# A four-block graph network on one core: node stages pipelined by tile and laid beside the passes over the edges

## The reference, cut to what matters

```python
# block 0: messages
s, v = x[:, :32] @ lin1_s, einsum(x[:, 32:], lin1_v)        # node product
w = silu(edge_attr_8 @ fc1) @ fc2                            # per edge, 8 -> 64 -> 128
ns, nv = segment_sum(products of w, s[src], v[src], edge_attr_4, by dst)
out = concat([ns @ lin2_s, nv @ lin2_v])                     # node product
# block 1: three convolutions with layernorm and elu, then a fourth
c = segment_sum((h @ W)[src] * dinv[src] * dinv[dst], dst) + b
h = elu(layernorm(c * sigmoid(a)) * g + beta)
# block 2: mean over neighbours, by src
mean = segment_sum(x[dst], src) / max(count, 1)
out = relu(x @ W_self + b_self + (mean @ W_neigh + b_neigh if count > 0))
# block 3: attention with two heads
e = leaky_relu(a_src[src] + a_dst[dst]); alpha = softmax of e over the edges of a dst
out = prelu(segment_sum((x @ W_src)[src] * alpha, dst) + bias)
```

## Time and profile before

| | |
|---|---|
| median of 3 runs | 10167.17 us (10166.1 to 10173.07) |
| the profiled execution | 10193.51 us, span 10191.7 us |
| PE busy | 6004.4 us (59%) |
| DVE busy | 5701.8 us (56%) |
| ACT busy | 2635.3 us (26%) |
| POOL busy | 6861.4 us (67%) |
| mean granted TensorE clock | 0.779 |
| HBM traffic | 75 GB/s over the span |

### The profile page before, as it was taken

One profiled execution on the slowest core, in us unless ns is written; L12 is line 12 of the kernel. 1 busy time (PEld: TensorE's weight loads), 2 busy tenths in 40 slices (PEclk: granted clock), 3 DMA queues, 4 the chain that ended last, 5 costly groups with the idle time before them and its releaser, 6 DMA issues. The chain is left out here.

```text
span 10191.7 us, 104956 instructions
## 1 busy us (share of the span) xinstructions
PE 6004.4 (59%) x23343; PEld 4243.9 (42%) x23343; DVE 5701.8 (56%) x15117; ACT 2635.3 (26%) x8724; POOL 6861.4 (67%) x7083
## 2 busy tenths in 40 slices
PE   0676745555766665666656666555554443477775
PEld 0343423333544443444434444333343333366664
DVE  9306047777455556555565555544443333599998
ACT  0332345555222223111121111100010000366663
POOL 0677757777177774777657775577767777177774
PEclk9999977777588886888878888777765555688886
DMA  7111123334022232333323333333332222222222
GB/s 260 50 58 48 58 76 99 102 102 91 25 52 52 52 50 73 100 101 101 83 85 100 100 100 72 94 101 100 100 78 52 53 52 52 35 48 48 48 48 39
DMA packets 350525, 773.48 MB, mean 76 GB/s; under 512 B 120740, under 2 KB 181816, under 8 KB 343336
## 3 DMA queue, kind: packets, MB, share of 16 engines
q0 software_dynamic: 251328, 600.99, 23.9%
q1 hardware_dynamic: 91176, 108.80, 3.8%
q10 hardware_dynamic: 7488, 57.94, 1.5%
HBM read 615.60 MB, written 151.68 MB: 75 GB/s over the span
## 5 line engine op out<-in xcount | busy, mean ns | idle before, releaser
L573 DVE TENSOR_TENSOR acc<-acc,ps 128x256 f32 (+3 forms) x4992 | 1886.4, 378 | 2885.3 <-PE ps L870 2430.2
L870 PE MATMUL ps<-rows,hot 128*128 128x256 f32 (+2 forms) x5824 | 1651.9, 444 | 1792.6 <-issue 947.9
L749 POOL DMA_INDIRECT rows<-table_gcn,index_dst x2080 | 2078.7, 999 | 676.2 <-issue 600.8
L870 PEld LDWEIGHTS ps<-rows,hot 128*128 128x128 f32 x5824 | 1285.6, 273 | 2226.2 <-issue 1232.7
L791 ACT ACTIVATE ut<-u,fld 128x128 f16<-128x128 f16 x1664 | 576.7, 393 | 2757.7 <-DVE u L828 2756.5
L749 POOL DMA_INDIRECT rows<-table_gat,index_dst x832 | 923.0, 1109 | 464.5 <-issue 253.2
L492 POOL DMA_INDIRECT dst_rows<-pay,acc x782 | 798.6, 1021 | 529.6 <-ACT pay L476 305.4
L749 POOL DMA_INDIRECT rows<-table_lin,index_dst x832 | 872.8, 1049 | 335.0 <-issue 239.5
L749 POOL DMA_INDIRECT rows<-table_mean,index_src x832 | 803.7, 966 | 258.4 <-issue 253.3
L725 PE MATMUL ps<-prod,hot 128*128 128x260 f32 x1664 | 626.4, 541 | 559.4 <-issue 365.5
L856 PE MATMUL ps<-prod,ut 128*128 128x416 f16 x3328 | 888.6, 399 | 0.0
(11 more groups left out here) (259 smaller groups left out, 9274.3 us busy)
## 6 DMA issues: line engine op xcount, KB each, us to landing
dst_rows<-pay ACTq DMA_DIRECT2D x52, 1088.0 KB, 31.5
fld<-dst_rows SPq DMA_DIRECT2D x104, 544.0 KB, 3.7
rows<-table_gcn,index_dst POOLq DMA_INDIRECT x2080, 2.5
table_gcn<-acc SPq DMA_DIRECT2D x15, 1024.0 KB
rows<-table_lin,index_dst POOLq DMA_INDIRECT x832
rows<-table_mean,index_src POOLq DMA_INDIRECT x832, 2.5
rows<-table_gat,index_dst POOLq DMA_INDIRECT x832
dst_rows<-pay,acc POOLq DMA_INDIRECT x782, 2.3
```

The source lines that it names most:

```text
L573: c.nc.vector.tensor_tensor(to, to, product, ALU.add).then_inc(c.added.sem, 1)
L749: pool.indirect_dma_start(to(q, j), None, table, bass.IndirectOffsetOnAxis(ap=c.idx[k][:, t:t + 1], axis=0)).then_inc(c.gathered[q % per]. ...
L870: pe.matmul(c.ps[:, j % ahead, 0:used], c.hot[:, r % 2, j, :], row_of(c, s, r, j, used), start=True, stop=True).then_inc(c.mm.sem, 1)
```

## The change

1. **Scatter.** `scatter_dst` takes on the first node product, one tile per group of eight chunks, for the first 49 groups. SP's order becomes load of group q, store of tile q-1 into t0, load of group q+1. PE turns tile q ahead of the group's layers and multiplies tile q-1 behind them. ACT copies tile q back (`back`) and tile q-1 out (`take`) behind its payload copies. The node product and `write_table` behind the stage are gone.
2. **Messages to first convolution.** `degrees`, the node product, `normalise` and `ranges` become `message_glue`: `turn_tiles` with two halves and one 128-row weight matrix (`apart`), norm per cut on ACT, degree root by Newton steps on POOL, table per cut by SP. The message rows are 257 wide (`AU`) instead of 260.
3. **Roots.** `newton` has three iterations instead of four, for every cut root; `CUTS` has 45 where it had 46, `conv_glue` shifts by `due(k, 3)` and joins at the cut's fifth tile instead of its last.
4. **Mean.** `aggregate` by src also makes `x @ W_self + b_self` into `acc[:, tile, 132:260]`, turning or multiplying one tile on PE in alternate groups; sums use four PSUM banks instead of eight. SP sends the bins of the chunks through HBM, and DVE makes of them the penalties that `bin_starts` made.
5. **Mean to attention.** `mean_glue` runs everything from the mean's product to table t6 in one stage of 67 steps (49 tiles + `ROWS`): the norm of tile k-14, its turn at k-16, product at k-17, rows at k-18. POOL also clears `acc` by cut.
6. **Attention.** The destination's scores are listed once for all chunks (two transposes, four matmuls against a one-hot of the bins, four copies), and `node_scores` is one copy of eight chunks.
7. **End.** `add_gat` and `normalise` become `final_glue`: ACT divides by the sum of weights, DVE adds bias, prelu, x and statistics per cut, POOL the root, ACT the norm, SP the store, per cut.

The core of the diff:

```diff
+            def put(k, h):
+                sp.wait_ge(m.taken.sem, k + (m.taken.n + 1))
+                sp.dma_start(to[:, one(k), :], s.u[:, h:h + 1, 0:D]).then_inc(m.put[h].sem, 16)
+
+            def both(i, h):
+                load(i, h, G8)
+                if not (first(i) and h == 0):
+                    put(2 * i + h - 1, 1 - h)
...
+            with sp.Fori(1, half // 2) as i:
+                for h in range(2):
+                    both(i, h)
...
+            def turn(k, h):
+                if not (isinstance(k, int) and k < 2):
+                    pe.wait_ge(m.back.sem, k + (m.back.n - 1))
+                pe.transpose(c.ps[:, 4 + h, 0:P], c.x[:, one(k), :].rearrange("p a w -> p (a w)"),
+                             c.ident[:, :]).then_inc(m.turned.sem, 1)
+
+            def multiply(k, h):
+                pe.wait_ge(m.back.sem, k + (m.back.n + 1))
+                if not (isinstance(k, int) and k < 2):
+                    pe.wait_ge(m.taken.sem, k + (m.taken.n - 1))
+                pe.matmul(c.ps[:, 6 + h, 0:D], s.ut[:, h, 0:P], s.lin1[:, :], start=True,
+                          stop=True).then_inc(m.multiplied.sem, 1)
+
+            def both(i, h):
+                q = 2 * i + h
+                turn(q, h)
+                mlp(i, h, G8)
+                if q:
+                    multiply(q - 1, 1 - h)
...
+            def back(k, h):
+                act.wait_ge(m.turned.sem, k + (m.turned.n + 1))
+                if not (isinstance(k, int) and k < 2):
+                    act.wait_ge(m.multiplied.sem, k + (m.multiplied.n - 1))
+                nc.scalar.activation(s.ut[:, h, 0:P], c.ps[:, 4 + h, 0:P], ACT.Copy).then_inc(m.back.sem, 1)
+
+            def take(k, i, h):
+                act.wait_ge(m.multiplied.sem, k + (m.multiplied.n + 1))
+                if not (isinstance(k, int) and k < 2):
+                    act.wait_ge(m.put[h].sem, i * 16 + m.put[h].n)
+                nc.scalar.activation(s.u[:, h, 0:D], c.ps[:, 6 + h, 0:D], ACT.Copy).then_inc(m.taken.sem, 1)
+
+            def both(i, h):
+                q = 2 * i + h
+                payload(i, h, G8)
+                back(q, h)
+                if not (first(i) and h == 0):
+                    take(q - 1, i - (h == 0), 1 - h)
...
+            def own(k):
+                dve.wait_ge(m.multiplied.sem, m.multiplied.n + k + 1)
+                nc.vector.tensor_tensor(c.acc[:, k, OWN:OWN + D], c.ps[:, 6 + k % 2, 0:D], s.bself[:, :],
+                                        ALU.add).then_inc(m.taken.sem, 1)
...
+                if bins is not None and q % 2 == 0 and 2 <= q < 2 * NT + 2:
+                    own(q // 2 - 1)
+                if bins is not None and q == 9:
+                    penalties()
...
+            def turn(k):
+                if k >= 2:
+                    pe.wait_ge(m.back.sem, m.back.n + k - 1)
+                pe.transpose(c.ps[:, 4 + k % 2, 0:P], c.x[:, k, :], c.ident[:, :]).then_inc(m.turned.sem, 1)
+
+            def multiply(k):
+                pe.wait_ge(m.back.sem, m.back.n + k + 1)
+                if k >= 2:
+                    pe.wait_ge(m.taken.sem, m.taken.n + k - 1)
+                pe.matmul(c.ps[:, 6 + k % 2, 0:D], s.ut4[:, k % 4, 0:P], s.wself[:, :], start=True,
+                          stop=True).then_inc(m.multiplied.sem, 1)
...
+def newton(st, y, of, e):
+
+    eng = st.eng
+    for i in range(3):
+        st(eng.tensor_tensor(e, of, y, ALU.mult)).wait()
+        st(eng.tensor_tensor(e, e, y, ALU.mult)).wait()
+        st(eng.tensor_scalar(e, e, -0.5, 1.5, ALU.mult, ALU.add)).wait()
+        last = eng.tensor_tensor(y, y, e, ALU.mult)
+        if i < 2:
             st(last).wait()
-    last.then_inc(s.m.rooted.sem, 1)
+    return last
...
-                for j in due(k, 2):
+                for j in due(k, 3):
                     shifted(j)
                 if i:
                     measure(k - 1)
-                if g >= 2 and k == CUTS[g + 1] - 1:
+                if g >= 2 and i == min(4, CUTS[g + 1] - CUTS[g] - 1):
...
+def message_glue(c, s, table):
+
+
+    nc = c.nc
+    v, m = nc.vector, s.m
+    node = lambda k: c.x[:, k, :]
+    with nc.Block() as block:
+
+        @block.tensor
+        def _(pe):
+            turn_tiles(c, s, pe, lambda k: c.acc[:, k, 0:HID], 2, s.lin2, 2 * MUL, 2, apart=True)
+
+        @block.scalar
+        def _(act):
+            def normal(k):
+                g, i = cut_of(k)
+                if i == 0:
+                    act.wait_ge(m.centred.sem, m.centred.n + g + 1)
+                nc.scalar.activation(node(k), node(k), ACT.Identity, scale=c.rstd[:, k:k + 1],
+                                     bias=c.mv[:, k, 0:1]).then_inc(m.part.sem, 1)
+
+            for k in range(NT):
+                bring_back(c, s, act, k, HID)
+                g, i = cut_of(k)
+                if g >= 2:
+                    n, of = CUTS[g + 1] - CUTS[g], CUTS[g - 1] - CUTS[g - 2]
+                    for j in range(i * of // n, (i + 1) * of // n):
+                        normal(CUTS[g - 2] + j)
+            for k in range(CUTS[NCUT - 2], NT):
+                normal(k)
+
+        @block.vector
+        def _(dve):
+            st = Steps(dve, c.dve)
+
...
+            for k in range(NT):
+                g, i = cut_of(k)
+                if i == 0 and g:
+                    measure(k - 1)
+                    cut_moments(c, s, st, g - 1, D, -1.0)
+                bank = 2 + k % 2
+                dve.wait_ge(m.multiplied.sem, m.multiplied.n + k + 1)
+                v.tensor_tensor(node(k)[:, 0:MUL], node(k)[:, 0:MUL], c.ps[:, bank, 0:MUL], ALU.add)
+                vec = node(k)[:, MUL:D].rearrange("p (u i) -> p i u", i=3)
+                v.tensor_tensor(vec, vec, c.ps[:, bank, MUL:D].rearrange("p (i u) -> p i u", i=3),
+                                ALU.add).then_inc(m.taken.sem, 1)
+                if i:
+                    measure(k - 1)
+                if g == 2 and i == 0:
+                    dve.wait_ge(m.back.sem, m.back.n + k)
+                    dve.wait_ge(m.fed.sem, m.fed.n + 2)
+                    st(v.tensor_scalar(s.ndinv[:, :], c.dinv[:, :], -1.0, None, ALU.mult))
+                if g >= 3 and i == 0:
+                    rows(g - 3)
...
+            pool.wait_ge(m.fed.sem, m.fed.n + 1)
+            newton(st, c.dinv[:, :], s.degree[:, :], s.newton[:, :]).then_inc(m.fed.sem, 1)
+            pool.wait_ge(m.fed.sem, m.fed.n + 2)
+            for g in range(NCUT):
+                t = slice(CUTS[g], CUTS[g + 1])
+                cut_root(c, s, st, g)
+                pool.wait_ge(m.rooted.sem, m.rooted.n + g + 1)
+                pool.tensor_tensor(c.mv[:, t, 0], c.mv[:, t, 0], c.rstd[:, t], ALU.mult).then_inc(m.centred.sem, 1)
...
+NORMAL, TURN, MULTIPLY, ROWS = 14, 16, 17, 18
...
+            turn(0)
+            turn(1)
+            for k in range(NT + ROWS):
+                if k < NT:
+                    multiply(k)
+                if k + 2 < NT:
+                    turn(k + 2)
+                if 0 <= k - TURN < NT:
+                    turn_node(k - TURN)
+                if 0 <= k - MULTIPLY < NT:
+                    multiply_node(k - MULTIPLY)
...
+            for k in range(NT + ROWS):
+                if k < NT:
+                    back(k)
+                if 0 <= k - NORMAL < NT:
+                    normal(k - NORMAL)
+                if 0 <= k - ROWS < NT:
+                    rows(k - ROWS)
+                if 0 <= k - TURN < NT:
+                    node_back(k - TURN)
...
+            def take(k):
+                dve.wait_ge(m.multiplied.sem, m.multiplied.n + k + 1)
+                v.scalar_tensor_tensor(part(k), c.ps[:, 2 + k % 2, 0:D], s.rcnt[:, k:k + 1], c.acc[:, k, OWN:OWN + D],
+                                       ALU.mult, ALU.add).then_inc(m.taken.sem, 1)
+
+            def bias(k):
+                dve.wait_ge(m.taken.sem, m.taken.n + k + 1)
+                v.scalar_tensor_tensor(part(k), s.bneigh[:, :], s.has[:, k:k + 1], part(k), ALU.mult,
+                                       ALU.add).then_inc(m.shifted.sem, 1)
+
+            def residual(k):
+                dve.wait_ge(m.shifted.sem, m.shifted.n + k + 1)
+                v.scalar_tensor_tensor(node(k), part(k), 0.0, node(k), ALU.max, ALU.add).then_inc(m.cut.sem, 1)
+
+            def measure(k):
+                dve.wait_ge(m.cut.sem, m.cut.n + k + 1)
+                st(v.bn_stats(s.st6[:, k, :], node(k)))
+                g = cut_of(k)[0]
+                if k == CUTS[g + 1] - 1:
+                    cut_moments(c, s, st, g, D, -1.0)
...
+                pool.wait_ge(m.taken.sem, m.taken.n + CUTS[g + 1])
+                pool.memset(c.acc[:, t, :], 0.0)
...
+            act.wait_ge(m.fed.sem, m.fed.n + 1)
+            divided(0)
+            divided(1)
+            for g in range(NCUT):
+                if g + 2 < NCUT:
+                    divided(g + 2)
+                normal(g)
...
+            for g in range(NCUT + 1):
```

(34 more changed lines are left out.)

519 lines of the change are left out of this document (343 added, 176 removed).

## The result

The changed kernel took 9930.3 us (median of 4, 9927.1 to 9931.8), the kernel before 10166.6 in the same comparison: a ratio of 0.9766, 95% interval 0.9749 to 0.9783, 236 us less. Forecast were 9933 and 234 less. The two profiled executions differ by more, 10193.5 and 9927.1, spans 10191.7 and 9925.3: 266 us. The one of before was 26 us over its median, the one of after was not. Totals are therefore compared only within one chip or with before on it, and stages first of all on the chip that gave 10164 for before.

The account below looks back on a forecast made before the run. POOL's indirect DMA issues bound each pass, and stages between passes add their length. Terms 72-51-112-24-2+3-98+0-22 = -234 took the profiled 10193.5 us to 9959, less 26 to the median: 9933 us, range 9865 to 9990.

Parts of the forecast that it names:

- the last one of the sum: Whole kernel: 9959 us for a profiled execution, lowered by the 26 us it lay above the median, to 9933.
- The chain: Scatter: tile copies, store, next load, TensorE and payload copies in series, 11.8 us a group for 50 groups, +72 us.
- my estimate of waits and register steps: Scatter, per group: waits and register steps on SP and ACT, store's packets ahead of the load's, 0.45 us.
- The rival of the hidden chain: Scatter: TensorE at its higher level, chain some 8 us, pass stays at 1045, total 9861 us; chance 0.15.
- The rival on TensorE's clock: New stages after the messages and the mean: TensorE stays at 1.2 GHz, +17 and +25 us, total 9975; chance 0.10.
- The likely case: Messages to first convolution: TensorE not at its lower level, 66.5 us to the first gather, -112 us.
- no memsets (-1): Messages to first convolution: the new stage lacks the memsets of the one after the fourth convolution, 1 us less.
- the stage loses one iteration and one tile of tail work: After the fourth convolution: one root iteration fewer and one tile of tail work shifted, -2 us.
- Step and stall: Mean to attention: 1.25 us a step, and ACT standing 2.7 us for the root at six cuts, 16 us.
- POOL waits for nobody in it, so one copy for eight on DVE gives 0 there: Pass of attention: copying the scores once for eight chunks gains 0 us, bounds -15 to +15.
- waits 0.3: End: DVE's waits per eight tiles, 0.3 us of 7.9, in a stage of 63.6 us, -22 us.
- the rival of the blocked roots: Root steps on POOL blocked by two-input DVE work, 2 to 4 us more at each of 13 cuts, 9965 us; chance 0.07.

Follow-up runs that it names:

- three orders at once: Changed kernel with SP's load ahead of the store in the scatter, norm three steps later after the mean, division ahead at the end: 9833.5 us, 0.9677 of before.
- the two runs above: Changed kernel with four root iterations and eight score copies: 9978.0 us; changed kernel with the old shift and join order, own product left out: 9937.1 us.

## Why the prediction was right, point by point

**The total was right partly by two errors that met.** The terms of the sum made 234 us where the traces have 266. The other step that failed is the last one of the sum, which took the 26 us between the profiled execution and the median of before as an offset that the changed kernel would have too. Its profiled execution had none (it was 3 us under its median), so the medians differ by 266 - 26 - 3 = 236. Seven gains were a little timid, the scatter's price, the gap after it and the end too hopeful; that the one made up for the other is luck. How much of the 26 us lies inside the timid terms is open; the gap after the mean may hold some, as before has 203.1 and 205.0 us there on the slower chips and 211.3 in the first profile.

**The scatter: right in mechanism, and in size within 9 us.** The chain, its order, POOL waiting for ACT and the end at group 50 came as forecast; the group was 12.04 for 11.8, and 50 x 0.24 = 12 us is about the difference. In the group shown the pieces come to the forecast's 11.8: 0.34 us for ACT's copies, 0.18 to the store's issue, 0.69 to the load's, 1.92 to TensorE's start and 8.62 from there, 11.75. The mis-sized piece is my estimate of waits and register steps. It left out the end of SP's loop, which makes every second group 0.6 us longer: by 0.1 to the store's issue, 0.3 to the load's and 0.2 to TensorE's start. The Trainium skill's section that the prediction names beside this sum ("DMA: Bandwidth & Descriptors", Anatomy of one DMA) is about DMAs that GpSimd issues, and this load is SyncE's; for it the trace's own 1.86 to 2.19 us stand. The rival of the hidden chain was the wrong picture of a right thought: TensorE did not run faster (it was at its lower level throughout), but one line of SP's order hides the chain completely, as three orders at once shows.

**The gap after it** -48 for -51: between the copies behind the scatter and the memsets 3.1 us of the block's start remain (1424.59 to 1427.65), which the forecast had struck out with the product.

**Messages to first convolution** -120 for -112. The rival on TensorE's clock is real and is drawn anew in each execution: the same 326 matmuls took 49.55 us busy at 0.81 in the first profile, and 72.23 at 0.56 in the window of the three orders, with the stage 14 us longer. That is at 0.56; carried on to 0.50, the lower of its levels (1.2 GHz), it makes some 17 us, my estimate from these two, which is what the rival said. The argument against it, 128-row operands for 64, decided nothing: both executions have them. The likely case was the other. The recorded terms of the stage add up to some 69 us and not to the 66.5 taken, and the stage took 58.6 from the last sum (2591.2) to the next pass (2649.9). The size that failed is most likely "no memsets (-1)": in the stage that it was modelled on, the one after the fourth convolution, memsets take 11.3 us of POOL's time and stand between its roots (see below). No run isolates this.

**Convolution stages** -30 for -24: the wait fell by 34, and I had taken 24. Showing which part did it needed the two runs above.

**After the fourth convolution** -8.5 for -2. The failed step is "the stage loses one iteration and one tile of tail work": the iteration alone is worth 7.0 there, because POOL paces this stage, root and memset following one another. From the second profile of the changed kernel:

```profile
7464.23 0.20 POOL L1324 TENSOR_TENSOR newton<-mv,rstd 128x8 f32<-128x8 f32 x1 [1.48 <-DVE rstd L1310]
...
7468.83 1.83 POOL L1623 MEMSET acc<- 128x2080 f32 x1
7471.41 0.20 POOL L1324 TENSOR_TENSOR newton<-mv,rstd 128x8 f32<-128x8 f32 x1 [0.75 <-DVE rstd L1310]
```

From one cut's root to the next it is 7.17 us, and 7.9 to 8.3 with four iterations, so every cut adds its own.

**Pass of the mean** -6 for +3: the own product costs nothing; why the pass is shorter than in the one profile of before is open.

**Mean to attention** -108 for -98. Step and stall were about right: 1.24 us for 1.25, and ACT's wait for the root 12.9 us for 16 (10.1 in the second profile), which three more steps of distance took away for 5.8 us net. What was too dear are the first 14 steps, priced like the others although they have no norm, turn or second product yet: 11.8 us for 17.5.

**Attention** -9.6 for 0. The failed step is "POOL waits for nobody in it, so one copy for eight on DVE gives 0 there": it did not wait, but its issues were longer, and eight copies for one put 8.8 us back.

**The end: half of the forecast,** -11 for -22. The step that failed is "waits 0.3" in the 7.9 us per cut: DVE stood 14.3 us for ACT's divisions, 4 of it at the start. (49 tiles at that rate are also 48.4 us and not 49.5.) Four rows of the changed kernel, beside one of the stage's roots:

```profile
9867.39 1.22 DVE L1885 TENSOR_TENSOR x<-x,hot_v 128x1024 f32<-128x1024 f32 x1
9867.56 1.11 POOL L1324 TENSOR_TENSOR newton<-mv,rstd 128x8 f32<-128x8 f32 x1 [51.08 <-DVE rstd L1310]
9868.64 1.23 DVE L1872 TENSOR_TENSOR hot_v<-hot_v,bias 128x1024 f32<-128x1024 f32 x1
9868.75 1.18 POOL L1325 TENSOR_TENSOR newton<-newton,rstd 128x8 f32<-128x8 f32 x1
```

A root step of 0.20 us ends with the wide DVE operation beside it, four of the twelve steps of this root: 3.6 us. That is the rival of the blocked roots. It is strongest here; in the stage after the fourth convolution it is one step in most roots, as before the change. L1324 has 743 ns in the mean over 15 here, and 226 in the stage after the mean, whose DVE operations are 128 wide. ACT stood 26.3 us for these roots, with the next divisions queued behind the wait, and so DVE stood for the divisions. "SBUF - State Buffer" in the Trainium skill (SBUF: two separate sides) has this lock, and this trace agrees; by these rows the price goes with the width of DVE's operations. Putting the division ahead gave 9.5 and 12.7 us back and left DVE 4.0 us of its wait, though the blocked step grew longer still (934 ns in the mean with the three orders, for 743): the order, not the lock by itself, was the price.

## What to carry to other kernels

Work that is laid beside a stage is not free because its engines are: count the queue that its DMAs join, and never put a load that was issued ahead behind a store that waits for this turn's work. Changing that order alone was worth 80 us. In a small chain on GpSimd beside wide two-input VectorE work a step can last as long as the VectorE operation that it meets (here four steps of twelve, 1.1 us for 0.20), so put nothing behind its wait that VectorE will want. And take forecasts from stages of a trace, but compare totals in medians: one profiled execution can lie off by a tenth of the change.

## What the runs showed of the hardware that was not expected

Chips differ: before took 10164 us on one and 11604 to 11636 on three others, with the stages between the passes nearly as long and the passes 8 to 38% longer (attention 1610 and 1619 for 1176 us), engines standing 1 to 5 us and more without a releaser in the profile. The ratio of the two kernels stayed within 0.002, but what one part of the change, the first, was worth turned its sign.

The granted clock of one and the same stage, the one after the messages, was 0.81, 0.70 and 0.56 in three executions, and its length followed: 82.8, 86.0 and 96.8 us.
